# Window attention stage: score quads in two pairs, one maximum and one exponential over a pair's two PSUM banks, and four engines' work in another order

## What is computed

```python
# _L0_conv_ref, called on _gn(x): windows of 8x8 = 64 tokens, 8 heads of 16 channels
xn = (win - mu) * rsqrt(var + 1e-5) * ln_gamma + ln_beta      # LayerNorm over 128 channels
q, k, v = split(xn @ w_qkv.T + b_qkv)
scores = einsum('nhqd,nhkd->nhqk', q / 4, k)
attn = softmax(scores, axis=-1)
o = einsum('nhqk,nhkd->nhqd', attn, v) @ w_out.T + b_out
x = x + o
```

## Time and profile before

| | us |
|---|---|
| median of 3 runs | 2669.88 |
| lowest, highest | 2667.43, 2674.15 |
| the profiled execution | 2671.07 |
| its span in the profile | 2669.1 |
| busy in the span: PE, DVE, ACT, POOL | 2468.9, 2159.1, 2157.9, 1716.4 |

### The profile page before, as it was taken

The page is one execution under the profiler, slowest core; times in us unless marked ns, Lnnn a source line. Parts: engine busy times, 40 slices in busy tenths (PEclk is TensorE's granted clock), DMA queues, the critical chain, the costliest instruction groups (busy, mean ns, idle before and its releaser), DMA issues.

```text
span 2669.1 us, 107195 instructions
## 1 busy us (share of the span) xinstructions
PE 2468.9 (92%) x43420; PEld 2088.9 (78%) x43420; DVE 2159.1 (81%) x4875; ACT 2157.9 (81%) x4093; POOL 1716.4 (64%) x1714
## 2 busy tenths in 40 slices
PE   3888789888888899899989999999999999999999
PEld 2666566666666667688978988898898899889888
DVE  6888788888988888667788888888888888888885
ACT  2777567766777777566779999999999999999998
POOL 2555445544555455366647777777777777777778
PEclk9999899999999999899989999999999999999999
DMA  4222122212221111144401101111110111100000
GB/s 151 70 76 72 51 82 76 75 59 78 78 74 53 48 55 49 50 136 127 138 15 42 41 32 42 42 42 38 42 42 32 42 41 42 39 28 21 17 21 25
DMA packets 55794, 152.18 MB, mean 57 GB/s; under 512 B 6608, under 2 KB 20944, under 8 KB 55632
## 3 DMA queue, kind: packets, MB, share of 16 engines
q1 hardware_dynamic: 55632, 149.93, 17.3%
HBM read 98.52 MB, written 51.38 MB: 56 GB/s over the span
## 4 chain that ended last, share of the span: by engine, by line
PE 72%; DVE 18%; issue 4%; ACT 2%; POOL 2%; DVEq 0%; SPq 0%; DMA 0%; POOLq 0%; ACTq 0%
PE bank L1285 17%; PE bank L1287 17%; PE bank L1286 17%; DVE mx L967 7%; PE bank L1440 6%; PE bank L1339 4%; DVE vx L960 3%; PE bank L1507 3%; PE bank L1302 2%; ACT prob L674 2%; DVE gst L835 2%; PE bank L1350 1%; DVE xc L953 1%; PE bank L1453 1%; POOL lnrs L526 1%
## 5 line engine op out<-in xcount | busy, mean ns | idle before, releaser
L613 POOL TENSOR_TENSOR hl<-hf,hh 128x448 fp32r<-128x448 f32 x896 | 1025.2, 1155 | 307.5 <-ACT hf L796 301.3
L795 ACT ACTIVATE hh<-bank,fc1i 128x448 fp32r<-128x448 f32 x896 | 584.9, 653 | 67.1 <-PE bank L1287 61.4
L1168 DVE SCALAR_TENSOR_TENSOR bank<-oring,dw,bank 128x448 f32<-128x448 f32 x896 | 614.9, 686 | 20.0
L796 ACT ACTIVATE hf<-bank,fc1i 128x448 f32<-128x448 f32 x896 | 586.2, 654 | 0.0
L1285 PE MATMUL bank<-t1h,w_hi 128*128 128x448 f32 x896 | 365.6, 408 | 5.9 <-DVE t1l L1187 5.6
L1285 PE MATMUL bank<-hh,w_hi 128*128 128x448 f32 x896 | 328.2, 366 | 0.0
L1287 PE MATMUL bank<-hl,w_hi 128*128 128x448 f32 x896 | 327.9, 366 | 0.0
L1287 PE MATMUL bank<-t1l,w_hi 128*128 128x448 f32 x896 | 327.4, 365 | 0.0
L1286 PE MATMUL bank<-hh,w_lo 128*128 128x448 f32 x896 | 327.2, 365 | 0.0
L1286 PE MATMUL bank<-t1h,w_lo 128*128 128x448 f32 x896 | 326.6, 365 | 0.0
L532 POOL TENSOR_TENSOR xn_lo<-xn,xn_hi 128x512 fp32r<-128x512 f32 x112 | 128.7, 1149 | 252.0 <-ACT xn_hi L651 252.0
(11 more groups left out here) (167 smaller groups left out, 5966.4 us busy)
## 6 DMA issues: line engine op xcount, KB each, us to landing
ximg<-x SPq DMA_DIRECT2D x112, 448.0 KB, 3.4
ximg<-x_in SPq DMA_DIRECT2D x56, 448.0 KB, 3.4
x<-ximg SPq DMA_DIRECT2D x56, 448.0 KB, 2.5
y_out<-yb SPq DMA_DIRECT2D x112, 224.0 KB, 1.9
xs<-x_in SPq DMA_DIRECT2D x42, 448.0 KB, 3.4
wm<-wm_in SPq DMA_DIRECT2D x1, 512.0 KB, 5.3
w1f<-w_in SPq DMA_DIRECT2D x1, 512.0 KB, 8.8
w<-w_in SPq DMA_DIRECT2D x1, 512.0 KB, 9.6
```

What stands on the lines that cost most here:

```text
L613: g.tensor_tensor(hl[:, k, :], hf[:, k, :], hh[:, k, :].bitcast(F32), ALU.subtract).then_inc(hl_ready, 1)
L795: a.activation(hh[:, j, :], p, ACT.Gelu, bias=bias)
L796: a.activation(hf[:, j, :], p, ACT.Gelu, bias=bias).then_inc(hf_ready, 1)
L1168: m = d.scalar_tensor_tensor(acc, src, dw[:, k:k + 1], acc, ALU.mult, ALU.add)
```

## The change

It touches the attention stage alone.

- Banks 0 and 1 become one PSUM tensor, duo[0], banks 2 and 3 another, duo[1]. The four quads are worked as two pairs, h = 0 and h = 1. `maxima` is two reductions, each over the two banks of a pair; `exps` is two exponentials, each over the two banks of a pair. The total of elements is the same.
- `score_rows` and `score_cols` run for one pair at a time. `score_cols` takes pair 1 first, then `project_q`, then pair 0, and the exponentials follow in that order. `project_k` now stands ahead of all of it.
- prob has two buffers.
- `project_v` makes 2 x 2 x pairs matmuls of 64 columns of the stationary operand and 64 moving columns, the even heads into partitions 0 to 63 and the odd heads into 64 to 127 of bank 4; its weights are a reordered copy, wvs. `v_evac` is two copies instead of four, and they stand apart on DVE.
- Output transposes and the output projection use bank 6 in place of bank 4, the transposed maxima bank 7 in place of bank 6.
- The order of the steps on PE, DVE, ACT and POOL is another.

```diff
-        bank = [ctx.enter_context(nc.psum_tensor(f"bank{n}", [P, 512], F32)) for n in range(8)]
+        duo = [ctx.enter_context(nc.psum_tensor(f"duo{h}", [P, 2, 512], F32)) for h in range(2)]
+        bank = [duo[n // 2][:, n % 2, :] for n in range(4)] + \
+               [ctx.enter_context(nc.psum_tensor(f"bank{n}", [P, 512], F32)) for n in range(4, 8)]
...
-            def exps(G, gg):
+            def exps(G, gg, h):
...
-                act.wait_ge(st_mm, G + 1)
-                for j in range(QUADS):
-                    m = a.activation(prob[:, j, 0:n // 64].rearrange("p w q -> p (w q)"), bank[j][:, 0:n], ACT.Exp)
-                m.then_inc(prob_ready, 1)
+                act.wait_ge(st_mm[h], G + 1)
+                a.activation(prob[:, gg, 2 * h:2 * h + 2, 0:n // 64].rearrange("p j w q -> p j (w q)"),
+                             duo[h][:, :, 0:n], ACT.Exp).then_inc(prob_ready[h], 1)
...
-            def v_evac(G, gg):
+            def v_evac(G, gg, e):
+                n = GROUP_PAIRS[gg]
                 dve.wait_ge(v_mm, G + 1)
-                for dst, src in value_blocks(gg):
-                    m = d.tensor_copy(dst, src)
-                m.then_inc(v_ready, 1)
+                src = bank[4][64 * e:64 * e + 64, 0:P * n].rearrange("p (w j d) -> p w j d", j=QUADS, d=HD)
+                d.tensor_copy(vx[64 * e:64 * e + 64, gg, 0:2 * n, :, (HD + 1) * e:(HD + 1) * e + HD], src)\
+                    .then_inc(v_ready, 1)
...
-            def maxima(G, gg):
+            def maxima(G, gg, h):
                 n = GROUP_PAIRS[gg]
-                dve.wait_ge(smax_mm, G + 1)
-                for j in range(QUADS):
-                    m = d.tensor_reduce(mx[:, gg, 32 * j:32 * j + 2 * n],
-                                        bank[j][:, 0:P * n].rearrange("p (e k) -> p e k", k=64), AX.X, ALU.max)
-                m.then_inc(max_ready, 1)
+                dve.wait_ge(smax_mm[h], G + 1)
+                dst = mx[:, gg, 64 * h:64 * h + 64].rearrange("p (j e) -> p j e", j=2)[:, :, 0:2 * n]
+                d.tensor_reduce(dst, duo[h][:, :, 0:P * n].rearrange("p j (e k) -> p j e k", k=64), AX.X, ALU.max)\
+                    .then_inc(max_ready, 1)
...
             def project_v(G, gg):
-                for t in range(GROUP_PAIRS[gg]):
-                    c = slice(P * t, P * t + P)
-                    m = mm(bank[7][:, c], xn[:, gg, c], wmat("wv"), start=True, stop=True)
+                for w in range(2 * GROUP_PAIRS[gg]):
+                    for e in range(2):
+                        m = mm(bank[4][64 * e:64 * e + 64, 64 * w:64 * w + 64], xn[:, gg, 64 * w:64 * w + 64],
+                               wvs[:, e, :], start=True, stop=True)
                 m.then_inc(v_mm, 1)
```

DVE's step in the new order (the helpers are those of before):

```diff
+                for h in range(2):
+                    maxima(G, gg, h)
                 if near(2):
                     ln_stats(G + 2, gg)
+                mt_evac(G, gg)
...
                 if near(-1):
+                    normalise(G - 1, ng, 1)
                     normalise(G - 1, ng, 0)
+                if near(1):
+                    v_evac(G + 1, ng, 0)
+                if near(2):
+                    ln_norm(G + 2, gg)
                 if gg == 1 and near(-2):
                     strip_stats(*strip_back(i, s), G - 1)
-                if near(2):
-                    ln_norm(G + 2, gg)
                 if near(1):
-                    v_evac(G + 1, ng)
+                    v_evac(G + 1, ng, 1)
```

PE's step in the new order, from the transposed maxima on:

```diff
+                transpose_maxima(G, gg)
                 if near(-1):
                     attend(G - 1, ng, 0)
...
-                transpose_maxima(G, gg)
                 if near(1):
                     pe.wait_ge(xnl_ready, G + 2)
+                    if near(-2):
+                        pe.wait_ge(ob_ready, G - 1)
+                    project_k(G + 1, ng)
+                score_cols(G, gg, 1)
+                if near(1):
                     if near(-1):
                         pe.wait_ge(oh_ready[1], G)
                     project_q(G + 1, ng)
-                    if near(-2):
-                        pe.wait_ge(ob_ready, G - 1)
-                    project_k(G + 1, ng)
-                score_cols(G, gg)
+                score_cols(G, gg, 0)
                 if near(1):
-                    pe.wait_ge(q_ready, G + 2)
+                    pe.wait_ge(k_ready, G + 2)
                     project_v(G + 1, ng)
                 if near(2):
                     ln_back(G + 2, gg)
```

More of the change, by code:

```diff
@@ L105, in build @@
         qb = sb("qb", [P, NIMG])
+        wvs = sb("wvs", [P, 2, P // 2])
         pws = [sb(f"pw_{n}", [P, 2, P], F32R) for n in ("hi", "lo")]
@@ L172, in build @@
         tstl = sb("tstl", [P, 2, STRIP], F32R, stack_b)
+        stack_p = ExitStack()
+        prob = sb("prob", [P, 2, QUADS, 8, 64], F32, stack_p)
+        stack_p.close()
         kv = sb("kv", [P, 2, 4, 2, 2, P], F32, stack_b)
@@ L237, in build @@
         k16_ready = sem("k16_ready")
-        smax_mm = sem("smax_mm")
+        smax_mm = [sem(f"smax_mm{n}") for n in range(2)]
         max_ready = sem("max_ready")
@@ L241, in build @@
         mt_ready = sem("mt_ready")
-        st_mm = sem("st_mm")
-        prob_ready = sem("prob_ready")
+        st_mm = [sem(f"st_mm{n}") for n in range(2)]
+        prob_ready = [sem(f"prob_ready{n}") for n in range(2)]
         pv_mm = sem("pv_mm")
@@ L377, in ring_copies, with quad_pair @@
                    ([(0, BLOCK_ROWS - 1)] if u == 3 and after else [])
[L379 to L387, removed]
+        def quad_pair(h):
+            return range(2 * h, 2 * h + 2)
         def hold(eng):
@@ L681, in ot_evac @@
                 act.wait_ge(ot_mm, G + 1)
-                a.activation(ot[:, gg, 0:n], bank[4][:, 0:n], ACT.Identity, bias=v("bv")).then_inc(ot_ready, 1)
+                a.activation(ot[:, gg, 0:n], bank[6][:, 0:n], ACT.Identity, bias=v("bv")).then_inc(ot_ready, 1)
             def ob_evac(G, gg):
@@ L1307, in quad_rows, with score_rows @@
                 return slice(32 * j, 32 * j + 32)
-            def score_rows(G, gg, reuse):
+            def score_rows(G, gg, h, reuse):
                 pe.wait_ge(q16_ready, G + 1)
@@ L1337, in score_cols @@
                     for s in range(2):
-                        for j in range(QUADS):
+                        for j in quad_pair(h):
                             m = mm(bank[j][64 * s:64 * s + 64, 64 * w:64 * w + 64], kx[quad_rows(j), gg, w, s, :],
                                    qs[quad_rows(j), gg, w, :], start=False, stop=True, skip_group_check=True)
-                m.then_inc(st_mm, 1)
+                m.then_inc(st_mm[h], 1)
             def attend(G, gg, h):
@@ L1381, in step @@
                 norms = at_norms(i, s) and gg == 0
-                score_rows(G, gg, near(-1))
+                if gg == 0:
+                    score_rows(G, gg, 0, near(-1))
                 if near(-2):
                     out_transpose(G - 2, gg)
-                pe.wait_ge(v_ready, G + 1)
+                if gg == 1:
+                    score_rows(G, gg, 0, near(-1))
+                score_rows(G, gg, 1, near(-1))
                 if near(-1):
@@ L1414, in epilogue @@
             def epilogue():
-                pe.wait_ge(ob_ready, NG - 2)
                 out_transpose(NG - 2, 0)
-                pe.wait_ge(prob_ready, NG)
-                pe.wait_ge(v_ready, NG)
+                for h in range(2):
+                    pe.wait_ge(prob_ready[h], NG)
+                pe.wait_ge(v_ready, NG * 2)
                 attend(NG - 1, 1, 1)
```

58 lines of the change are left out of this document (29 added, 29 removed).

## The result

| | before | after |
|---|---|---|
| median of the runs | 2671.28 us (4) | 3036.85 us (4) |
| lowest, highest | 2667.43, 2674.15 | 3031.68, 3040.97 |
| profiled execution, its span | 2671.07, 2669.1 | 3031.68, 3029.9 |
| ratio | | 1.1369, 95% interval 1.1344 to 1.1393 |

The account below looks back on a forecast made before the run. Neither PE nor DVE is full; who waits for whom sets the pace, and the new order makes them take turns. 2671.1 + 194 (strips) + 72 (last image) + 50 (clock) - 20 (shared), 1 less: 2965 us, range 2860 to 3040.

Parts of the forecast that it names:

- PE's legs: TensorE's work from transposed maxima to the next values, forecast at 5.9 us in an even and 5.9 in an odd group.
- the clock: New PE waits of 1.9 to 2.0 us bring one half-clock stretch of 3.4 us a strip, 0.9 us net, 50 us.
- The savings: Merged maxima and value copies on DVE: 1.0 us less work in a strip.
- the wait for the exponentials: The 0.55 us that score_rows waits on PE, claimed to go and counted as gain.
- DVE's legs: DVE's work from the values to the next group's maxima: 5.4 us even step to odd group, 5.9 odd to even.
- the second rival: Half clock in every group of the attention stage: 50 us more, 3015 us, chance 0.13.
- The last image: Strips without statistics of a next image: 22.9 us instead of 17.77, 14 of them, 72 us.
- The 20 us shared with disturbed strips: Of 52 us in strips disturbed by group-norm coefficients and image changes, 20 taken off as shared with the new waits.
- Free pairs: Score pairs at no cost and no half clock: 2863 us, chance 0.15.
- Doubled scores: Scores at half of the array take double time: 101 us more, 3066 us, chance 0.06.
- Merged instructions as dear as what they replace: A merged instruction over two banks costs as much as the two replaced: 56 us more, 3021 us, chance 0.05.
- Faster: The loop does not close, the copies wait for nothing, both engines run at their own work: 2653 us, chance 0.04.

Follow-up runs that it names:

- e2: Kernel before with two of the four value copies put ahead of ln_norm on DVE, nothing else: 2879.82 us, 1.0788 of before.
- e1: Changed kernel with ln_norm put back ahead of the first copy of the values on DVE: 2846.17 us, 1.0657 of before.
- e4: Kernel before, its order kept, with merged maxima and exponentials, project_v in two column halves and two value copies instead of four: 2626.25 us, 0.9834 of before.
- e8: Kernel of e4 with out_transpose ahead of score_rows on PE: 2624.17 us, 0.9831 of before.
- e3: Changed kernel with eight useless matmul passes of 384 columns between project_v and ln_back in each group: 2965.41 us, 1.1105 of before.
- e5: Kernel before with score_cols cut in pairs, each with its selection passes, nothing between: 2774.26 us, 1.0396 of before.
- e7: Kernel before with merged maxima and exponentials alone, values and every order as before: 2653.91 us, 0.9937 of before.
- e6: Kernel of e1 with the scores of all four quads uncut, behind the q projection: 2745.47 us, 1.0284 of before.
- e9: Kernel of e4 with half of attend behind the transposed maxima, normalise behind mt_evac, k projection ahead of q: 2681.21 us, 1.0033 of before.
- e10: Kernel of e3 with four useless passes in place of eight: 2974.20 us, 1.1143 of before.

## Why the prediction came out as it did

The mechanism was right: a copy that waits for `project_v` ahead of `ln_norm`, PE idle until xc, two engines taking turns. e2 makes 210 us of loss with that edit alone, e1 takes back 191 of the 366 by undoing that edit alone. The sizes of two terms, PE's legs and the clock, were too small and one deduction had nothing behind it. The steps one by one:

- **What bounds the kernel.** Right: the order, not an engine's work. DVE has less to do and the stage is 34% longer.
- **The savings.** Right in size: maxima of a group 2.36 and 1.82 (2.30 and 1.77 forecast), a copy 0.68 and 0.55 (0.70 and 0.57). e4 shows them worth 44 us when the order lets them count. I called the wait for the exponentials part of the gain; by e8 and by the rows it was worth nothing, and the sum had put nothing on it.
- **DVE's legs.** 5.45 us for 5.4 in the even step. The other leg, in a strip of after that no group-norm step disturbs, runs from the first copy at 590.23 to the end of the maxima at 593.69 + 2.36 = 596.05, 5.82 us for the forecast 5.9:

```profile
590.23 0.68 DVE L966 COPY vx<-bank 64x512 f32<-64x512 f32 x1 [4.21 <-PE bank L1312]
...
593.69 2.36 DVE L973 TENSOR_REDUCE mx<-duo 128x16 bf16<-128x1024 f32 x2
```

- **PE's legs, mis-sized.** From the transposed maxima to the values at DVE: 330.76 - 324.46 = 6.30 and 342.37 - 336.27 = 6.10, where the forecast legs without the waking are 5.85 each. The missing 0.7 us a strip is in two terms. A pair's scores take 1.09 and 0.86 us, where the sum had 1.02 and 0.79: the 16 passes between the two take 0.23, 14.4 ns a pass, as estimated from one tile (56 ns by four), and what is left, 0.17, is the change-over, taken as 0.12 from the selection. And the projections were taken from rows where three passes follow three passes (0.62, 0.78); k takes 326.24 - 325.54 = 0.70. The first pass of such a run behind other work takes 0.25 us to the next (325.54 to 325.79), behind another run 0.18 (662.06 to 662.24 in the trace of before); why is not shown. In both legs and both pairs that makes 0.28 and 0.38 us. 0.7 x 56 = 39 us. e3's strip of 23.60 for 23.1 agrees with most of it.
- **The clock, mis-sized.** I took one stretch of half clock a strip. The stage has about 370 us at half clock, some 330 more than before, where one stretch of 3.4 us in each of 56 strips makes 190. So it is nearly two a strip (330/190 = 1.7), close to the count of the second rival; its net price by e3 is 71 us at least, for the 50 that I took (and 100 of the rival). The doubt was placed rightly (waits of 1.9 us between 1.49, which kept the clock, and 2.14, which did not); the side was the worse one. The last image shows it too: the sum had 22.9 us a strip, and DVE's maxima of after, at 1339.56, 1366.22 and 1390.75, are 26.66 and 24.53 us apart (23.47 in e3, so 0.6 of it is not the clock):

```profile
1339.56 2.39 DVE L973 TENSOR_REDUCE mx<-duo 128x16 bf16<-128x1024 f32 x2
...
1366.22 2.36 DVE L973 TENSOR_REDUCE mx<-duo 128x16 bf16<-128x1024 f32 x2
...
1390.75 2.39 DVE L973 TENSOR_REDUCE mx<-duo 128x16 bf16<-128x1024 f32 x2
```

- **The 20 us shared with disturbed strips.** Not seen. e3's stage runs from 47.6 to 1415.1 us, 1367, and 56 strips of 23.6 make 1322. Those 46 us, and the 9 of the last groups behind the last `score_rows` that the 52 include (1077 for 1115.9 - 47.5 = 1068), are as much beside the steady strips as before. The term should have been nothing.
- Together 39 + 21 + 20 = 80 against the 72 us missed. All three err to the same side. That the median still lies inside, by 3 us, is in part luck: the upper end was set by rivals, and one of them, half clock in every group, came nearly true. That e3 (2965.4) equals the forecast is chance. The sum as written gives 2967 - 1 = 2966; the forecast says 2965.
- **The rivals.** Free pairs: refuted by e5 (104 us). Doubled scores: 2 x 1.09 for 1.52 us is 1.43 times. The Trainium skill, TensorEngine Tiling (Array Packing), section Theoretical Speedup, gives a factor of up to 4 for a small dimension of 32 or less; taken in proportion to the tiles, as the rival did, it would be 2 times here, which this trace does not show for L1339; the measurement decides. Merged instructions as dear as what they replace: refuted by e4 and e7. Faster: refuted, the loop closed, as the copies wait 4.40 and 3.86 us.

The account by experiments, from the changed kernel down: 3037, less 191 (the order on DVE, with its clock) is e1 2846; less 101 (the cut scores) is e6 2745. From the other side: e4 2626, plus 55 (half of `attend` and `normalise` behind the maxima, k first) is e9 2681. Between 2681 and 2745 lie 64 us that no run takes apart: e6 differs from e9 in `score_rows` in two pieces, the copies on both sides of the finished strip's statistics (`strip_stats`), the statistics behind the wait for the values, other banks for the outputs, and the order on ACT and POOL. The traces show where most of it lies. Of DVE, first e6, then e9:

```profile
425.30 0.68 DVE L966 COPY vx<-bank 64x512 f32<-64x512 f32 x1 [1.73 <-PE bank L1312]
425.90 1.14 DVE L836 BATCH_NORM_STATS2 gst<-ximg  x2
```

```profile
422.26 1.15 DVE L839 BATCH_NORM_STATS2 gst<-ximg  x2
...
425.31 1.39 DVE L968 COPY vx<-bank 64x512 f32<-64x512 f32 x2 [0.95 <-PE bank L1310]
426.74 2.36 DVE L976 TENSOR_REDUCE mx<-duo 128x16 bf16<-128x1024 f32 x2
```

In e9, as before, the statistics of the finished strip fill the wait for the values; in e6, as in the changed kernel, they stand behind the first copy. So from the first copy to the maxima e6 takes 427.79 - 425.30 = 2.49 us and e9 1.43, 1.06 us more of the strip's 1.08 (19.65 for e9's 18.57), and 56 x 1.06 = 59 of the 64 us. This is read from traces; no run moves the statistics alone. It is the same error of order as the copy ahead of `ln_norm`: work whose inputs are ready was taken out of a wait. e5 and e6 agree on the cut from both sides, 104 and 101 us.

## What to carry to other kernels

Before an instruction that waits for another engine is put ahead of one that the other engine will wait for, ask who feeds whom: work whose inputs are ready belongs into the wait, ahead of it. Fewer, longer instructions pay only what lies on the path (44 us here) and one exchanged pair in the order costs four to five times that (191 and 210 us); make the two changes apart. When TensorE gets a new idle time in every round, price the granted clock too, and try a few useless matmuls in the gap to see what it costs.

## What the runs showed of the hardware beyond what was expected

- Useless matmul passes in a gap made the kernel 2.3% faster (2965.4 for 3036.9 us; granted clock of the stage 0.97 for 0.87), and half as many did nearly as much (2974.2, 0.96).
- Scores on four tiles of 32 by 64 instead of eight take 1.09 us for 64 passes, 17 ns a pass, for 11.9 ns on eight: 1.43 times. Each run of passes has 0.16 to 0.17 us that does not go with their number; without it a pass takes 14.4 ns on four tiles (1.09 - 0.86 for 16) and 10.6 on eight (1.52 - 1.18 for 32), 1.35 times.
- A wait of 1.69 us was followed by half clock for 13.6 us in e10, in which PE was busy 13.25 us, and by full clock in e3: the length of the wait alone does not say what the clock does.
- A reduction or an exponential over two PSUM banks in one instruction costs no more than its elements: reductions 2.36 us for 2 x 1024 columns, 2.48 for 4 x 512; exponentials 1.94 (e7) for 2 x 1024 and 2.06 (before) for 4 x 512.
